# Rotary q and k rotated straight from PSUM with the sum on GpSimd, ternary raw weights stored elsewhere, fewer stacking transfers, new order tables

## The reference

```python
x = x + 0.5 * L0_ffn(layernorm(x))         # gate, up, down as integers minus 128, with scales; silu(gate) * up
x = x + L0_attn(layernorm(x))              # 16 heads of 16, rotary q and k, causal softmax
x = x + 0.5 * L0_ffn(layernorm(x))
x = x + 0.5 * L1_ffn(layernorm(x))         # weights rounded to -1, 0, 1; sigmoid(x w1) * (x w2), then w3
x = x + L1_attn(layernorm(x))              # 16 query heads, 4 key heads, ALiBi bias, causal softmax
x = x + 0.5 * L1_ffn(layernorm(x))

def _apply_rope(x, cos, sin):
    x1, x2 = (x[..., :half], x[..., half:])
    return jnp.concatenate([x1 * cos - x2 * sin, x2 * cos + x1 * sin], axis=-1)
```

## Time and profile before

| | us |
|---|---|
| median of 3 runs (lowest, highest) | 648.75 (646.61, 649.05) |
| the profiled execution | 647.0 |
| its span, first to last instruction | 645.2 |
| PE busy in the span | 578.3 (90%) |
| DVE, ACT, POOL busy | 477.6, 405.6, 253.2 |
| mean granted TensorE clock | 0.974 |

### The profile page before, as it was taken

The page is one execution under the profiler, slowest core; times in us unless marked ns, Lnnn a source line. Parts: engine busy times, 40 slices in busy tenths (PEclk is TensorE's granted clock), DMA queues, the critical chain, the costliest instruction groups (busy, mean ns, idle before and its releaser), DMA issues.

```text
span 645.2 us, 14201 instructions
## 1 busy us (share of the span) xinstructions
PE 578.3 (90%) x5770; PEld 314.8 (49%) x5770; DVE 477.6 (74%) x806; ACT 405.6 (63%) x644; POOL 253.2 (39%) x279
## 2 busy tenths in 40 slices
PE   2798985888969998999999999999998997999986
PEld 1355542544533553556545465556554543555553
DVE  4789899987797779785867776886866676763442
ACT  5846645357765486665866756675857657767542
POOL 7674777320153327225223541335244012032433
PEclk9989999889988999999999999999999899999999
DMA  9500033231143013401230103010301141101200
GB/s 341 237 1 2 1 49 61 39 50 38 37 68 66 2 36 62 75 9 26 50 60 10 36 9 74 18 21 18 62 1 36 21 79 37 36 35 34 71 35 33
DMA packets 18577, 31.84 MB, mean 49 GB/s; under 512 B 6176, under 2 KB 7584, under 8 KB 18232
## 3 DMA queue, kind: packets, MB, share of 16 engines
q1 hardware_dynamic: 18512, 30.94, 20.5%
HBM read 13.75 MB, written 2.36 MB: 25 GB/s over the span
## 4 chain that ended last, share of the span: by engine, by line
PE 45%; DVE 13%; DMA 10%; POOL 9%; ACT 8%; issue 8%; SPq 5%; POOLq 0%; DVEq 0%; ACTq 0%
PE PS L518 11%; PE PS L547 8%; PE PS L637 7%; DMA RB<-scratch 5%; PE PS L597 4%; PE PS L619 3%; DVE MX L941 3%; POOL HH L1018 3%; ACT PB L767 3%; SPq L433 2%; PE PS L469 2%; DMA scratch<-DC 2%; PE PS L652 2%; PE PS L496 2%; POOL OC L1046 2%
## 5 line engine op out<-in xcount | busy, mean ns | idle before, releaser
L767 ACT ACTIVATE PB<-PS 128x1024 f32<-128x1024 f32 x160 | 160.3, 1018 | 61.9 <-PE PS L469 61.0
L941 DVE TENSOR_REDUCE MX<-PS 128x2 f32<-128x1024 f32 (+2 forms) x192 | 158.4, 862 | 47.1 <-PE PS L469 46.8
L518 PE MATMUL PS<-XT,WGU 128*128 128x512 f16 x640 | 160.1, 391 | 3.6 <-DVE XT L872 1.7
L1018 POOL TENSOR_TENSOR HH<-TH,HH 128x512 f16<-128x512 f32 (+1 forms) x96 | 104.7, 1098 | 147.8 <-ACT HH L726 147.6
L518 PEld LDWEIGHTS PS<-XT,WGU 128*128 128x128 f16 x640 | 56.3, 99 | 73.2 <-issue 10.6
L469 PE MATMUL PS<-MASKM,MASKW 64*128 64x128 bf16 (+1 forms) x1280 | 83.0, 207 | 0.0
L547 PE MATMUL PS<-WD,HH 128*128 128x256 f16 x640 | 78.2, 276 | 2.9 <-POOL HH L1018 2.5
L637 PE MATMUL PS<-PB,V 128*32 128x512 f32 (+3 forms) x1024 | 76.4, 439 | 2.2 <-ACT PB L767 2.2
L597 PE MATMUL PS<-SK,SQ 54*128 54x256 f16 (+3 forms) x512 | 63.5, 307 | 13.0 <-DVE TH L891 3.7
L726 ACT ACTIVATE HH<-TH 128x512 f16<-128x512 f32 (+1 forms) x96 | 55.3, 589 | 29.9 <-PE PS L547 10.5
L619 PE MATMUL PS<-SQ,SK 55*128 55x384 f16 (+3 forms) x512 | 62.6, 303 | 10.4 <-ACT PB L767 4.1
(11 more groups left out here) (92 smaller groups left out, 750.3 us busy)
## 6 DMA issues: line engine op xcount, KB each, us to landing
SQ<-QPB SPq DMA_DIRECT2D x48, 128.0 KB, 4.2
OC<-OT SPq DMA_DIRECT2D x64, 64.0 KB, 2.3
RB<-scratch SPq DMA_DIRECT2D x32, 128.0 KB
SK<-QPB SPq DMA_DIRECT2D x24, 128.0 KB, 4.7
out<-X SPq DMA_DIRECT2D x4, 512.0 KB, 2.8
PB<-wd SPq DMA_DIRECT2D x2, 768.0 KB, 10.7
PB<-gu SPq DMA_DIRECT2D x2, 704.0 KB, 6.0
PB<-gu SPq DMA_DIRECT2D x1, 1408.0 KB, 12.0
```

What stands on the lines that cost most here:

```text
L518: m = e.matmul(o[:, :], WGU[l][:, k, col:col + P], XT[0][j][:, k, :], start=first, stop=last)
L767: e.activation(PB[Q % 2][:, j, :, :], two_banks("s", i), ACT.Exp, scale=0.25).then_inc(a_exp, 1)
L941: e.tensor_reduce(MX[:, Q % 4, :, pr, t], o[:, :, col:col + (t + 1) * P], AX.X, ALU.max, negate=True).then_inc(a_max, 1)
L1018: e.tensor_tensor(HH[1][:, s * T:s * T + wd], TH[:, i % 3, 0:wd], HH[0][:, s * T:s * T + wd], ALU.subtract).then_inc(f_lo, 1)
```

## The change

The rotation no longer goes through ACT: the shuffle and the cosine product read q from its PSUM bank, the scale is folded into the table of cosines and sines, and the sum of both products goes from DVE (letter r) to POOL (new letter a). The low half of the context (C) goes from DVE to POOL too; its factor 16 is now in the value matrix's column of ones, which is 1/16. The heads' parts in SQ, SK, V and OT are interleaved over the partitions (every fourth, or every other one) where they were blocks, so that a stacking takes 3 transfers and not 6, and the copy of the context 1 and not 4. A contraction over the stacked rows has 63 and 64 rows, 54 and 55 before. The raw ternary weights and the intermediates lie in SQ[1] and SK[1], which the second attention unit fills; these are cleared on POOL behind the preparation (waits on p_dve 30) and not at the start. The third matrix of the ternary ones comes first and its scale is worked out apart (a second letter a on PE). The exponentials wait for less. All five strings and the banks are new; the multisets of letters are the same but for those named.

```diff
-        rgu = raw[1][:, 0:4 * HID].rearrange("p (k n) -> p k n", k=2)
-        rd = raw[1][:, 4 * HID:4 * HID + FC * D].rearrange("p (c n) -> p c n", c=FC)
+        rd = raw[1][:, 0:FC * D].rearrange("p (c n) -> p c n", c=FC)
+        late = [t[1][:, :, :].rearrange("p h t -> p (h t)").bitcast(F32) for t in (SQ, SK)]
+        rgu = [late[k][:, 0:2 * HID] for k in range(2)]
...
-        def wait_weights(w):
-
-            w.wait_ge(p_act, NSTEP["act"])
-            w.wait_ge(p_pool, NSTEP["pool"])
-            w.wait_ge(p_dve, NSTEP["dve"])
+        def wait_exp(w, Q, j):
+
+
+            if Q == 0:
+                w.wait_ge(p_act, 3)
+                if j == NS_T - 1:
+                    w.wait_ge(p_act, 9)
+                    w.wait_ge(p_pool, 10)
+            elif j < 2:
+                w.wait_ge(p_dve, 14)
...
-                    w.wait_ge(p_pool, 9)
+                    w.wait_ge(p_pool, (5, 15)[z])
                     w.wait_ge(a_qhi, last_chunk(i) + 1)
                     for blk, j in (((0, 0), (2, 0), (1, 1)) if is_q else ((0, 0), (1, 0), (2, 1))):
                         if j == 1:
                             wait_qlo(w, last_chunk(i))
-                        for a in range(2):
-                            r0 = 64 * a + 16 * blk
-                            e.dma_start((SQ if is_q else SK)[z][r0:r0 + 16, 0:ns, :],
-                                        QPB[a * width // 2:(a + 1) * width // 2, i % 2, j, 0:len(chunks), :]
-                                        ).then_inc(a_stk[0 if is_q else 1][z], 16)
+                        e.dma_start((SQ if is_q else SK)[z][blk:P:4, 0:ns, :], QPB[0:width, i % 2, j, 0:len(chunks), :]
+                                    ).then_inc(a_stk[0 if is_q else 1][z], 16)
...
-                    for a in range(4):
-                        e.dma_start(OC[32 * a:32 * a + 32, u, :],
-                                    OT[32 * a:32 * a + 16, 2 * u:2 * u + 2, :]).then_inc(t_oc[u], 16)
+                    e.dma_start(OC[:, u, :], OT[0:P:2, 2 * u:2 * u + 2, :]).then_inc(t_oc[u], 16)
...
-                elif c == "q":
-
-                    w.wait_ge(a_qk, i + 1)
-                    w.wait_ge(a_qlo[0], i - 1)
-                    e.activation(QF[:, i % 2, :], bank("q", i), ACT.Copy, scale=inv).then_inc(a_qf, 1)
...
                 elif c == "p":
-                    w.wait_ge(a_qf, i + 1)
+
+                    w.wait_ge(a_qk, i + 1)
                     w.wait_ge(a_rot, i - 1)
-                    e.stream_shuffle(QS[:, i % 2, :], QF[:, i % 2, :], [v ^ 4 for v in range(32)]).then_inc(a_sh, 1)
+                    e.stream_shuffle(QS[:, i % 2, :], bank("q", i), [v ^ 4 for v in range(32)]).then_inc(a_sh, 1)
                 elif c == "q":
                     w.wait_ge(l_c2, 48)
-                    w.wait_ge(a_sh, i + 1)
-                    e.tensor_tensor(QF[:, i % 2, :], QF[:, i % 2, :], ROPE[:, 0, :], ALU.mult).then_inc(a_cos, 1)
-                elif c == "r":
-                    w.wait_ge(a_cos, i + 1)
-                    w.wait_ge(a_sin, i + 1)
-                    e.tensor_tensor(QF[:, i % 2, :], QF[:, i % 2, :], QS[:, i % 2, :], ALU.add).then_inc(a_rot, 1)
+                    w.wait_ge(a_qk, i + 1)
+                    w.wait_ge(a_qhi, i - 1)
+                    w.wait_ge(a_qlo[0], i - 1)
+                    e.tensor_tensor(QF[:, i % 2, :], bank("q", i), ROPE[:, 0, :], ALU.mult).then_inc(a_cos, 1)
...
-                elif c == "C":
-                    n, u = divmod(i, 2)
-                    w.wait_ge(t_hi, i + 1)
-                    e.scalar_tensor_tensor(CH[1][:, u, :], OC[:, u, :], CS, CH[0][:, u, :], ALU.mult,
-                                           ALU.subtract).then_inc(t_lo, 1)
...
+                elif c == "a":
+                    w.wait_ge(a_cos, i + 1)
+                    w.wait_ge(a_sin, i + 1)
+                    e.tensor_tensor(QF[:, i % 2, :], QF[:, i % 2, :], QS[:, i % 2, :], ALU.add).then_inc(a_rot, 1)
...
+                elif c == "C":
+                    n, u = divmod(i, 2)
+                    w.wait_ge(t_hi, i + 1)
+                    e.tensor_tensor(CH[1][:, u, :], OC[:, u, :], CH[0][:, u, :], ALU.subtract).then_inc(t_lo, 1)
...
-        "kkkrrkrDrSRrDSrRrkDSRkrrDSrRkrkDSrRrlDSRrkkrDSrRrlDSRrkkrDSRrrDSRrkkrDSrRrDSrRkkrDSRrrDSRrOrDSRDSOR"
+        "kkrkrrkDSRrrDSRrrkDSRkrrDSRrkrkDSrRlrDSRrkkrDSRrlrDSRrkkDrSRrrDSRkrkrDSRrrDSRrkkDrSROrrDrSRrDSRrDSRO"
```

More of the change, by code:

```diff
@@ L378, in sync_program @@
             e.dma_start(BO[:, :], bo1).then_inc(l_a0, 16)
-            e.dma_start(rgu, gu1).then_inc(l_w1, 16)
-            e.dma_start(rd, wd1).then_inc(l_w1, 16)
+            e.dma_start(rd, wd1).then_inc(l_w3, 16)
+            for k in range(2):
+                e.dma_start(rgu[k], gu1[:, k, :]).then_inc(l_w1, 16)
             e.dma_start(X[:, 2 * NT:, :], x_in[:, 2 * NT:, :]).then_inc(l_x23, 16)
@@ L477, in tensor_program @@
                 if c == "a":
[L479 to L483 removed]
+                    wait_bank(w, "a", i)
+                    o = bank("a", i)
+                    w.wait_ge(p_pool, 7)
+                    w.wait_ge(p_dve, (7, 19)[i])
+                    c0, c1 = ((2, 3), (0, 2))[i]
+                    e.matmul(o[:, c0:c1], ONE, GS[:, c0:c1], start=True, stop=True).then_inc(p_pe, 1)
                 elif c == "t" or c == "u":
@@ new lines, in vector_program @@
+                        w.wait_ge(p_dve, 6)
+                        e.tensor_reduce(GS[:, 2:3], GA[:, 2, :], AX.X, ALU.add).then_inc(p_dve, 1)
+                    elif i in (4, 12):
+                        k = 0 if i == 4 else 1
+                        c0, c1 = ((2, 3), (0, 2))[k]
+                        w.wait_ge(p_pe, k + 1)
+                        e.tensor_scalar(GS[:, c0:c1], bank("a", k)[:, c0:c1], 1.0 / (HID * D), 1e-8,
+                                        ALU.mult, ALU.add).then_inc(p_dve, 1)
+                        w.wait_ge(p_dve, 8 + 12 * k)
+                        e.tensor_scalar(GS[:, 3 + c0:3 + c1], GS[:, c0:c1], -0.5, None, ALU.mult).then_inc(p_dve, 1)
+                        w.wait_ge(p_dve, 9 + 12 * k)
+                        e.tensor_scalar(GS[:, c0:c1], GS[:, c0:c1], 0.5, None, ALU.mult).then_inc(p_dve, 1)
+                    elif i <= 6:
+                        k = i - 5
+                        src = rd[:, 3 * k:3 * k + 3, :].rearrange("p c n -> p (c n)")
+                        w.wait_ge(p_dve, 10 + 2 * k)
+                        e.tensor_scalar(TD, src, GS[:, 5:6], None, ALU.is_lt).then_inc(p_dve, 1)
+                        w.wait_ge(p_dve, 11 + 2 * k)
+                        e.scalar_tensor_tensor(WD[1][:, 3 * k:3 * k + 3, :].rearrange("p c n -> p (c n)"), src, GS[:, 2:3],
+                                               TD, ALU.is_gt, ALU.subtract).then_inc(p_dve, 1)
+                    elif i <= 10:
+                        k, u = divmod(i - 7, 2)
+                        w.wait_ge(l_w1, 32)
+                        e.tensor_reduce(GA[:, u, 11 * k:11 * k + 11],
+                                        rgu[k][:, u * HID:(u + 1) * HID].rearrange("p (a b) -> p a b", b=64),
+                                        AX.X, ALU.add, apply_absolute_value=True).then_inc(p_dve, 1)
+                    elif i == 11:
+                        w.wait_ge(p_dve, 18)
+                        e.tensor_reduce(GS[:, 0:2], GA[:, 0:2, :], AX.X, ALU.add).then_inc(p_dve, 1)
+                    else:
+                        k = i - 13
+                        w.wait_ge(p_dve, 22 + 4 * k)
```

195 lines of the change are left out of this document (83 added, 112 removed).

## The result

The changed kernel took 602.19 us (median of 4 runs, 599.39 to 604.74), the one before 647.93 beside it: a ratio of 0.928, interval 0.925 to 0.931. The profiled execution took 603.93 us, its span is 601.9.

What follows compares the result with a forecast made beforehand. TensorE, busy 578.3 of 645.2 us, was taken as the bound, VectorE from 60 to 140 us. Gains of 21 less 1.5 took 647.0 to 627.5, 629 against the median; range 616 to 646.

Steps and rivals of the forecast that it cites:

- the sum: Whole kernel: gains of 8 + 3 + 6 + 3 + 1 = 21 us, less 1.5, so 19.5.
- Costed at nothing: Contractions of 63 or 64 rows, the second product for the scales, and the exponentials' dropped waits: no time counted.
- the part on the order: 60 to 140 us: gate and down products between the first m cut waits, within the same 8 us; clock gives 3.
- The bounds −5 and +9: 200 to 600 us: range around 3 us gained from many small waits, as new strings can be better or worse.
- 3 and about half of "6": Clock: 3 of 4.8 us lacking from 60 to 140; from 140 to 200, 6 of 8.6 idle and 5.4 clock.
- its clock terms: Gains from a less lowered clock: 3 us from 60 to 140, and a share of the 6 from 140 to 200.
- I leave the landing where it is and count only issues: Stacking transfers: landing kept at 4.2 us; only SyncE's fewer issues counted, and only from 140 to 200 us.
- the second rival: All 16 stackings and copies land sooner through every fourth partition: 6 to 10 us more, 621 us; chance 0.12.
- VectorE's relief: 60 to 140 us: eight rotation chunks free 12.2 us of VectorE, of which 8 us were taken as gain.
- 1.5: Loss in us for the preparation's instructions with two SBUF operands that now lie beside a fuller GpSimd.
- GpSimd did not take VectorE's place: Rival: GpSimd's in-order queue becomes the bound, the gain of 8 and 3 falls to about 2: 638 us; chance 0.16.
- the slower case: 60 to 140 us: GpSimd's queue delays clearings and later work, deciding above some 21 us idle: 659 us; chance 0.10.

Runs made afterwards that it cites:

- ungroup: The changed kernel with 66 swaps of neighbouring pieces in TensorE's string alone, raising changes of array shape from 310 to 442: 616.43 us.
- strings_before: The kernel before with all five strings and the banks ordered anew (not the changed kernel's strings), code and layout old, 307 changes of array shape: 611.90 us.
- undone: The changed kernel with old block layout and transfers, rotation's sum and low half back on VectorE, and TensorE's string at 442 changes of shape: 639.70 us.
- blocks: The changed kernel and its strings with the old block layout and so the old transfers, six for a stacking and four for a context copy: 620.32 us.
- split: The changed kernel, new layout kept, with each stacking transfer in two halves and each context copy in four: 613.38 us.
- strings_after: The changed kernel with other strings and banks only, all five ordered anew, 309 changes of array shape against 310: 597.95 us.
- strings_after_2: The changed kernel with a third set of strings and banks, pieces further behind what they wait for, 312 changes of array shape: 583.25 us.

## Why the prediction was wrong

- **The failed step** is one that the sum doesn't have. The part "Costed at nothing" and the part on the order took TensorE's 578.3 busy us as fixed; new strings could move waits only. The runs showed that the order sets busy time: 186 fewer changes at 0.10 us are 18.6 of the 26.3 us. The bounds −5 and +9 "the new strings can be better or worse at this, and no row tells" were too narrow. The trace of before had the row for it: behind four mask products of the same form the next product starts 0.21 us later where it goes over 128 rows (L547), and 0.12 us later where it is a half again (L597).

```profile
218.98 0.28 PE L469 MATMUL PS<-MASKM,MASKW 64*128 64x128 bf16 x4
219.19 1.26 PE L547 MATMUL PS<-WD,HH 128*128 128x256 f16 x10
...
221.26 0.28 PE L469 MATMUL PS<-MASKM,MASKW 64*128 64x128 bf16 x4
221.38 0.38 PE L597 MATMUL PS<-SK,SQ 54*128 54x256 f16 x4
```

- **The clock** was a second mis-sized term: 11 us of lacking clock went, 9.0 of them while TensorE was busy, where 3 and about half of "6" were taken. It isn't the main cause: ungroup had a still better clock and was slower, and strings_before gained 36 us without it. Nor did fewer changes or stops bring it: strings_before, with few of both, lacks 16.2 us, and undone, with many of both, 5.1. In every run on the old code the mean clock is 0.967 to 0.979, in every run on the changed code 0.983 to 0.999, whatever the strings, and with the old layout and VectorE's work back too. The prediction's reason, fewer stops, isn't borne out.
- **Waits**: 17.0 us less idle time is near the sum (some 15 without its clock terms), but placed otherwise. From 60 to 140 us TensorE still idles for 11.4 us (forecast: under 9) and VectorE is at 89% (under 85%).
- **Transfers**: "I leave the landing where it is and count only issues" was wrong in the first half and too small in the second. The issues counted in one stretch are worth about 11 us over the kernel. The landing did get shorter, as the second rival had it (0.12), but its 6 to 10 us aren't shown: blocks and split are 7 us apart, part of it the clock, with no difference in TensorE's idle time.
- **VectorE's relief** was the largest term, 8; its sum and low half are worth at most 6.5, within what placement does, and the cheaper cosine product was not tried alone. VectorE went to 448.0, not 441, 7 us that I had at 1.5; 3.0 of them are four instructions of the preparation (L866, one of them above with its 1.84 us; L853 before), which took 0.94 us each before. The three that overlap with GpSimd's work now took 1.84 to 1.95 us, and the fourth, at 88.0 us, where GpSimd is idle, 0.94.
- **Right**: cosine product, GpSimd's sum and total (285.8 for 293), 48 stackings, first m before 100 us, no wait of TensorE's that ends with L1034 or L1038. GpSimd did not take VectorE's place, and the slower case did not come, though GpSimd kept 80 − 55.6 = 24.4 idle us from 60 to 140, above the 21 from which I had let it decide: its idle time says nothing while nobody waits for it.

The direction came out as forecast and the sum of the waits with it, but 26.3 of the 43.3 us between the two profiled executions are busy time, for which the sum had only its clock terms, some 6 us.

What stays open: which part of the changed code raised the clock (undone keeps q read from its bank, the weights' new place and the shorter waits, and has the better clock); what the landing is worth; and why strings_after, with as few changes, gave 4 us where strings_after_2 gave 19 (idle time and stops fell in the second; which of its moves did it was not tried).

## What to carry to other kernels

When an order of instructions changes, count on TensorE where the array's shape changes between neighbours and how often it stops, before summing waits: busy time is not a constant of the program. Price a transfer by the issues that it puts into a queue ahead of others (96 of them were 11 us here) before its bytes. Split a change of busy time into changes of shape, stops and clock before you explain it. An edit's worth is that in its order: the same layout gave 8 us in one order and 18 in the other.

## What was unexpected of the hardware

A change between products over 128 rows and over halves of 64 rows cost 0.10 us, one to or from strips of 32 columns 0.11. A stop of TensorE added 0.16 us to its busy time in the profile. 128 KB to every fourth partition landed in 2.2 us, to blocks of 16 partitions in 4.2.
